# Attention with a ring of three PSUM pairs: another order of maxima and scores in rounds 3 to 5 of a unit

## The chip, the cores and the metric

The kernel runs on one core of a Trainium2 chip. The metric is the device time of one execution in microseconds (us), the median of the runs. The trace is one profiled execution. TensorE does matrix multiplies into PSUM, VectorE (DVE) and ScalarE (ACT) read PSUM and compute elementwise, GpSimd (POOL) works on SBUF alone, and SyncE (SP) issues the transfers. Each engine takes its instructions in order and waits on semaphores that others raise.

## What is computed

The reference is one block of a hybrid network on x of shape (2, 1024, 128):

```python
x = x + attention(layernorm(x))      # 16 heads of 64, causal; values are the keys; then @ W_out
x = x + mixture(layernorm(x))        # 16 experts of width 64, top 2, and a shared one
x = x + state_space(layernorm(x))    # inner width 256, 64 states, convolution of 3 taps, a scan
x = x + mixture(layernorm(x))

# attention, per batch and head
scores = (q / 8) @ k.T ; scores = where(causal, scores, -max)
attn = softmax(scores) ; out = attn @ k
```

The change touches only the attention, the first of the four stages.

## The kernel before

**Units.** `attention` (line 239) works in 16 units (`UNITS`). A unit is one pair of heads and one batch entry: 1024 queries by 1024 keys for two heads at once. The two heads lie in the two halves of the 128 partitions, so most matmuls come in pairs that run beside each other (x2 in the rows).

**What a unit needs.** The softmax subtracts a row maximum before the exponential. So each unit has two kinds of score computation. *Maxima* (`max_scores`, line 582, matmul on line 590) compute coarse scores with queries as rows, into PSUM, in ten fills M0 to M9 (`MAX_FILLS`). VectorE reduces each fill (`maxima`, line 488): where the fill crosses the diagonal it uses a scan with a mask for each head (line 498, followed by a small read of the accumulator), else one plain maximum (line 494). Maxima 2 and 5 are fills of 384 columns for each head, 1, 3, 4, 6, 7 and 9 of 512, 0 and 8 of 128 + 256. *Scores* (`scores`, line 603, matmuls on lines 616, 618, 620, 623, 625) compute exact scores with keys as rows, in nine fills S0 to S8 (`SLOTS`). The rows are high and low parts of queries and keys multiplied in three steps (616, 618, 620), a mask on diagonal tiles (623) and the subtraction of the row maximum (625). ScalarE takes the exponential of each fill (line 453). Maxima run one unit ahead: while unit u has its scores, unit u + 1 has its maxima.

**After the maxima.** `join_maxima` (line 504, instruction on line 507) reduces all maxima of a unit, TensorE turns the result (`turn_max`, line 595, matmul on line 600), and VectorE makes rows of it (line 512), which the scores of the next unit use.

**Rest of a unit.** Output matmuls (`outputs`, line 629, matmul on line 643) multiply the exponentials of the unit before by its keys, one burst at the start of each round. GpSimd adds up exponentials (line 378), TensorE turns the sums into denominators (`denominators`, line 649, matmul on line 656), at the start of rounds 2 and 4. Queries and keys of later units are projected (`project`, line 559, lines 567 to 569): queries in round 1, keys at the end of round 5. Keys are turned in round 1 (line 578).

**The ring.** Scores, maxima, projections and turned keys share one ring of three pairs of PSUM banks. `ring_uses` (line 223) lists all uses in the order of TensorE's work; use number i takes pair i modulo 3, and `pair_free` (line 286) makes TensorE wait until use i - 3 has been read: scores by ScalarE's exponential, maxima by VectorE, key projections by ScalarE.

**What sets the order.** The table `ROUNDS` (lines 211 and 212), written by hand. A unit has five rounds, one for each entry. TensorE, ScalarE and VectorE all walk through it; ScalarE takes the S entries, VectorE the M entries, TensorE both. In the last unit there are no M entries, since no unit follows. The output burst of a round comes before its row of the table.

Of the kernel before, what the change touches and what calls it, by code (L numbers as in the profile page):

```python
# [99 lines left out]
def layernorm_transposed(nc, s, k, load, banks, xn, sync_first, vector_first, gpsimd_work):  # L100
# [85 lines left out]
    def later(piece):  # L186
        def issue(eng):
# [20 lines left out]

BURSTS = [[(0, 0), (1, 0), (2, 0), (1, 1)], [(3, 0), (2, 1)], [(4, 0)], [(5, 0), (6, 0)], [(7, 0), (8, 0), (8, 1)]]
NBURST = len(BURSTS)  # L210
ROUNDS = [[("S", 0)], [("S", 1), ("M", 0), ("S", 2), ("M", 1)], [("S", 3), ("M", 2), ("S", 4), ("M", 3), ("M", 4)],
          [("S", 5), ("M", 5), ("S", 6), ("M", 6), ("M", 7)], [("M", 8), ("S", 7), ("M", 9), ("S", 8)]]
FIRST_OF_HALF = {0: 0, 1: 1}
BURST_OF = [max(r for r, b in enumerate(BURSTS) if any(s == slot for s, _ in b)) for slot in range(NSLOT)]

# [7 lines left out]
def ring_uses():  # L223

    uses = [("K", 0, 0), ("Q", 0, 0), ("T", 0, 0)] + [("M", 0, m) for m in range(NMAX)] + [("K", 1, 0)]
    for unit in range(UNITS):
        more = unit + 1 < UNITS
        for r, row in enumerate(ROUNDS):
            if r == 0 and more:
# [9 lines left out]
def attention(nc, k, w_qk, load_x, load_w_out):  # L239
# [3 lines left out]
    with Scope(nc, "at") as s:  # L243
# [113 lines left out]
        with nc.Block() as block:  # L357
# [57 lines left out]
            def _(act):  # L415
# [46 lines left out]
                for unit in range(UNITS):  # L462
                    more = unit + 1 < UNITS
                    for r, row in enumerate(ROUNDS):
                        if r == 0 and more:
# [15 lines left out]
            def _(dve):  # L481
# [50 lines left out]
                for unit in range(UNITS):  # L532
                    more = unit + 1 < UNITS
                    for r, row in enumerate(ROUNDS):
                        if r == 0:
# [22 lines left out]
            def _(pe):  # L558
# [112 lines left out]
                for unit in range(UNITS + 1):  # L671
                    more = unit + 1 < UNITS
                    for r, row in enumerate(ROUNDS):
                        if r == 0 and unit < UNITS:
# [987 lines left out]
```

How the kernel before makes its waits and increments, by code:

```python
def wait(eng, sem, value):  # L46
    if not isinstance(value, int) or value > 0:
        eng.wait_ge(sem, value)
# [32 lines left out]
def row_statistics(dve, stats, moments, x, small, count, done):  # L82
    for t in range(x.shape[1]):
        last = dve.bn_stats(stats[:, t, :], x[:, t, :])
    last.then_inc(small, 1)
    dve.wait_ge(small, count + 1)
    for t in range(x.shape[1]):
        last = dve.bn_aggr(moments[:, t, :], stats[:, t, :])
    last.then_inc(done, 1)
    return count + 1
# [26 lines left out]
    def norm(eng, n):  # L118
        eng.wait_ge(inverted, n + 1)
        scale_rows(eng, grp(xn, n), grp(k.x, n), grp(moments, n), cols(rstd, n), normed)
# [1 line left out]
    def turn(pe, n):  # L122
        pe.wait_ge(normed, n + 1)
        for j in range(PER):
            last = pe.transpose(tp[n % EARLY][:, j * P:(j + 1) * P], xn[:, n * PER + j, :], k.ident[:, :])
        last.then_inc(transposed, 1)
# [1 line left out]
    def high_part(act, n):  # L128
        act.wait_ge(transposed, n + 1)
        act.activation(k.xhi[:, n * BANK:(n + 1) * BANK], tp[n % EARLY][:, :], ACT.Copy).then_inc(high, 1)
# [1 line left out]
    def low_part(dve, n):  # L132
        dve.wait_ge(high, n + 1)
        c = slice(n * BANK, (n + 1) * BANK)
        dve.tensor_tensor(k.xlo[:, c], tp[n % EARLY][:, :], k.xhi[:, c].bitcast(FP32), ALU.subtract).then_inc(low, 1)
# [15 lines left out]
            def statistics(n):  # L151
                dve.wait_ge(x_loaded[n], 16)
                count[0] = row_statistics(dve, grp(stats, n), grp(moments, n), grp(k.x, n), small, count[0], varied)
```

## Time and profile before

| | before |
|---|---|
| median of 3 runs | 817.79 us (816.99 to 819.50) |
| profiled execution | 819.88 us |
| its span, first to last instruction | 818.1 us |
| mean granted clock of TensorE | 0.971 of full speed |
| TensorE busy (matmuls) | 746.5 us, 91% of the span |
| VectorE busy | 451.1 us, 55% |
| ScalarE busy | 386.0 us, 47% |
| GpSimd busy | 424.1 us, 52% |

The attention takes a bit less than the first 500 us of the span. Its sixteen units begin with the turned row maximum (line 600): unit 0 at 37.49 us, unit 6 at 209.58, unit 15 at 466.87. In the timelines a row gives the start in us from the begin of the span, the duration in us, the engine, line and operation, the tiles written and read, the shape, and how many instructions were merged into the row; in brackets the idle time of the engine before it and who ended it. A matmul's duration overlaps the next one's, so distances between starts tell more than durations. For weight loads (PEld) the list of waits has rows of its own.

### The profile page before, as it was taken

How to read it: one execution, taken by the hardware profiler on the slowest of the kernel's cores; microseconds unless marked ns; L12 is line 12 of the kernel's file. 1: busy time of each engine (PE TensorE's matmuls, PEld its weight loads, DVE VectorE, ACT ScalarE, POOL GpSimd, SP SyncE). 2: the span in 40 equal slices, each digit the busy share in tenths (PEclk: the TensorE clock that was granted, in tenths of full speed). 3: DMA queues.
4: the chain of work that ended last, by engine and by line, in shares of the span. 5: the costliest groups of instructions: out<-in, count | busy, mean ns of one | idle time of the engine just before them, and what ended most of it. 6: DMA issues, size and time to landing. Idle time of an engine off the chain costs nothing. (4 is left out here: it accounts for less than half of the span.)

```text
span 818.1 us, 14386 instructions
## 1 busy us (share of the span) xinstructions
PE 746.5 (91%) x5520; PEld 507.0 (62%) x5520; DVE 451.1 (55%) x1218; ACT 386.0 (47%) x476; POOL 424.1 (52%) x309
## 2 busy tenths in 40 slices
PE   2689999999999999999999998979799897779998
PEld 1456555655655565565556555958688763657887
DVE  5755665675567557556655701553554457555342
ACT  2346555555554555555455451355354344364421
POOL 4346775685676658658655862133544321144343
PEclk9789999999999999999999999999899899899999
DMA  2000000000000000000000004332222000033232
GB/s 64 8 1 1 9 1 1 8 1 1 9 1 2 7 1 2 8 1 2 1 2 26 1 2 101 92 105 78 69 80 90 1 1 0 1 111 112 71 100 78
DMA packets 29752, 25.56 MB, mean 31 GB/s; under 512 B 10162, under 2 KB 21236, under 8 KB 29684
## 3 DMA queue, kind: packets, MB, share of 16 engines
q1 hardware_dynamic: 29684, 24.64, 10.0%
q8 instruction: 44, 0.72, 0.4%
q14 instruction: 24, 0.20, 0.1%
HBM read 23.32 MB, written 1.31 MB: 30 GB/s over the span
## 5 line engine op out<-in xcount | busy, mean ns | idle before, releaser
L378 POOL TENSOR_TENSOR all_x<-all_x,at_probs 128x1024 f32<-128x1024 f32 (+3 forms) x128 | 221.7, 1732 | 35.7 <-ACT at_probs L453 21.1
L453 ACT ACTIVATE at_probs<-at_ring 128x1024 f32<-128x1024 f32 x144 | 147.2, 1024 | 113.6 <-PE at_ring L625 106.9
L498 DVE CUSTOM_DVE_ANT_0 at_ring<-at_ring,at_after_query 128x128 f32<-128x128 f32 (+3 forms) x256 | 119.5, 521 | 74.3 <-PE at_ring L590 74.3
L643 PE MATMUL at_out<-at_probs,at_k_nat 128*64 128x512 f32 (+3 forms) x768 | 140.3, 494 | 1.1 <-DVE a_attn_t L521 0.9
L1079 POOL TENSOR_TENSOR m_prod<-m_gate,m_wb 128x512 f32<-128x512 f32 x64 | 82.0, 1287 | 111.9 <-ACT m_gate L936 87.2
L378 POOL TENSOR_TENSOR all_x<-at_probs 128x768 f32<-128x768 f32 (+1 forms) x32 | 67.0, 2092 | 128.2 <-ACT at_probs L453 128.0
L990 DVE TENSOR_TENSOR m_hid<-m_prod,m_u 128x512 f32<-128x512 f32 x64 | 44.0, 687 | 90.0 <-POOL m_prod L1079 84.6
L643 PEld LDWEIGHTS at_out<-at_probs,at_k_nat 128*64 128x64 f32 x768 | 49.2, 136 | 69.9 <-issue 66.0
L494 DVE TENSOR_REDUCE at_half_max<-at_ring 128x2 f32<-128x1024 f32 x64 | 75.5, 1222 | 12.3 <-PE at_ring L590 12.3
L936 ACT ACTIVATE m_gate<-m_g 128x512 f32<-128x512 f32 x72 | 42.8, 598 | 81.9 <-PE m_g L847 81.5
L855 PEld LDWEIGHTS m_acc<-rest_wd,m_hid 128*128 128x128 f32 x576 | 76.7, 195 | 6.1
L616 PE MATMUL at_ring<-at_qh,at_kh 64*128 64x512 f32 (+3 forms) x384 | 73.6, 380 | 5.7 <-DVE at_m_rows L512 2.2
L855 PE MATMUL m_acc<-rest_wd,m_hid 128*128 128x128 f32 x576 | 76.8, 278 | 0.0
L625 PE MATMUL at_ring<-at_m_rows,at_ones_r 64*128 64x512 f32 (+3 forms) x384 | 75.9, 391 | 0.0
L590 PE MATMUL at_ring<-at_kh,at_qh 64*128 64x512 f32 (+3 forms) x384 | 64.2, 383 | 10.0 <-DVE at_half_max L498 3.0
L616 PEld LDWEIGHTS at_ring<-at_qh,at_kh 64*128 64x128 f32 x384 | 36.6, 187 | 52.6 <-issue 37.5
L618 PE MATMUL at_ring<-at_ql,at_kh 64*128 64x512 f32 (+3 forms) x384 | 66.9, 344 | 0.0
L620 PE MATMUL at_ring<-at_qh,at_kl 64*128 64x512 f32 (+3 forms) x384 | 66.8, 344 | 0.0
L590 PEld LDWEIGHTS at_ring<-at_kh,at_qh 64*128 64x128 f32 x384 | 35.9, 187 | 30.2 <-issue 26.8
L485 DVE TENSOR_TENSOR at_ql<-at_ring,at_qh 128x1024 fp32r<-128x1024 f32 x16 | 19.6, 1224 | 55.9 <-ACT at_qh L429 55.9
L444 ACT ACTIVATE at_inv<-at_misc 128x512 f32<-128x512 f32 x32 | 19.1, 598 | 65.3 <-PE at_misc L656 65.3
L620 PEld LDWEIGHTS at_ring<-at_qh,at_kl 64*128 64x128 f32 x384 | 36.4, 186 | 4.3
(218 smaller groups left out, 1289.4 us busy)
## 6 DMA issues: line engine op xcount, KB each, us to landing
m_wb<-m_wt_far SPq DMA_DIRECT2D x128, 128.0 KB, 2.9
all_x<-in_L_attn_a_x SPq DMA_DIRECT2D x8, 256.0 KB, 4.0
at_w_raw<-in_L_attn_a_W_qk SPq DMA_DIRECT2D x8, 128.0 KB, 2.6
out<-all_x SPq DMA_DIRECT2D x4, 256.0 KB, 3.3
a_room<-in_L_attn_a_W_out SPq DMA_DIRECT2D x1, 512.0 KB, 4.0
m_raw_wg<-in_L_ffn_experts_wg SPq DMA_DIRECT2D x1, 512.0 KB, 4.2
m_raw_wu<-in_L_ffn_experts_wu SPq DMA_DIRECT2D x1, 512.0 KB, 4.1
rest_wd<-in_L_ffn_experts_wd SPq DMA_DIRECT2D x1, 512.0 KB, 4.2
```

The costliest lines, as they stand in the source:

```text
L378: return pool.tensor_tensor(sums[:, :, a * P:b * P], left, right, ALU.add)
L453: act.activation(probs[:, :, slot * BANK:(slot + 1) * BANK], pair("S", unit, slot)[:, :, :], ACT.Exp, scale=BETA).then_inc(exp_done, 1)
L494: last = dve.reduce_max(half_max[:, :, i, out], pair("M", unit, m)[:, :, at:at + w], AX.X)
L498: last = dve.tensor_tensor_reduce(out=sums_ps, in0=sums_ps, in1=after_query[:, BANK - w:BANK], scale=1.0, scalar=MASKED, op0=ALU.add, op1= ...
L590: last = pe.matmul(out[:, l, at:at + (b - a) * P], qh[u][rows(l), i * P:(i + 1) * P], kh[u][rows(l), a * P:b * P], start=True, stop=True)
L616: pe.matmul(to[l], kh[u][rows(l), keys], qh[u][rows(l), q], start=True, stop=False)
L618: pe.matmul(to[l], kh[u][rows(l), keys], ql[u][rows(l), q], start=False, stop=False)
L620: pe.matmul(to[l], kl[u][rows(l), keys], qh[u][rows(l), q], start=False, stop=False)
L625: last = pe.matmul(to[l], ones_r[rows(l), :], m_rows[u][rows(l), q], start=False, stop=True)
L643: last = pe.matmul(out_ps[rows(l), o:o + (b - a) * P], k_nat[g % 3][:, j, rows(l)], probs[:, l, at:at + (b - a) * P], start=(j == 0), stop ...
L855: last = pe.matmul(acc[:, t * P:(t + 1) * P], hid[g % BUFS][:, t * P:(t + 1) * P], f.wd[:, st, :], start=(st == 0 and t == 0), stop=(st == ...
L1079: pool.tensor_tensor(prod[g % BUFS][:, :], gate[g % BUFS][:, :], wb[q % SPREAD][:, :], ALU.mult)\
```

## The change

Rounds 3 and 4 begin with a maxima fill instead of a scores fill, and in round 5 scores 7 go ahead of maxima 8. The instructions are the same, in the same number; `ring_uses` follows the table, so each fill's place in the ring and its wait follow too.

```diff
-ROUNDS = [[("S", 0)], [("S", 1), ("M", 0), ("S", 2), ("M", 1)], [("S", 3), ("M", 2), ("S", 4), ("M", 3), ("M", 4)],
-          [("S", 5), ("M", 5), ("S", 6), ("M", 6), ("M", 7)], [("M", 8), ("S", 7), ("M", 9), ("S", 8)]]
+ROUNDS = [[("S", 0)], [("S", 1), ("M", 0), ("S", 2), ("M", 1)], [("M", 2), ("S", 3), ("M", 3), ("S", 4), ("M", 4)],
+          [("M", 5), ("S", 5), ("M", 6), ("S", 6), ("M", 7)], [("S", 7), ("M", 8), ("M", 9), ("S", 8)]]
```

## Rows read from the trace of the kernel before

**Rows 1.** Busy time by window: us, then each engine, clock, DMA; unit 6.
```profile
210.00:238.75 28.75, 28.30 (x244) 16.58 (x240) 17.59 (x42) 15.63 (x19) 19.72 (x14) 1.00 0.02 6
```

**Rows 2.** List of waits, 40 to 520 us: us in total, times, longest.
```profile
PEld at_ring L616 <- DVE at_half_max L498: 9.5, 16, 1.0
...
PE at_ring L590 <- ACT at_probs L453: 2.6, 15, 0.3
```

**Rows 3.** Timeline (start, us, ..., idle before), TensorE, unit 6, rounds 2 and 3.
```profile
220.91 0.39 PE L590 MATMUL at_ring<-at_kh,at_qh 64*128 64x512 f32 x2
221.22 1.08 PE L643 MATMUL at_out<-at_probs,at_k_nat 128*64 128x512 f32 x4
222.23 0.50 PE L616 MATMUL at_ring<-at_qh,at_kh 64*128 64x512 f32 x2
222.57 0.40 PE L618 MATMUL at_ring<-at_ql,at_kh 64*128 64x512 f32 x2
...
223.28 0.34 PE L590 MATMUL at_ring<-at_kh,at_qh 64*128 64x384 f32 x2
...
224.68 0.79 PE L590 MATMUL at_ring<-at_kh,at_qh 64*128 64x512 f32 x4
225.40 1.94 PE L643 MATMUL at_out<-at_probs,at_k_nat 128*64 128x512 f32 x8
```

**Rows 4.** Timeline, VectorE, unit 6, rounds 2, 3 and 5.
```profile
222.63 0.14 DVE L498 DVE_READ_ACCUMULATOR2_ANT at_half_max<- 128x1 f32 x1
223.69 0.57 DVE L498 CUSTOM_DVE_ANT_0 at_ring<-at_ring,at_after_query 128x384 f32<-128x384 f32 x1 [0.92 <-PE at_ring L590]
...
224.69 0.14 DVE L498 DVE_READ_ACCUMULATOR2_ANT at_half_max<- 128x1 f32 x1
...
234.95 0.14 DVE L498 DVE_READ_ACCUMULATOR2_ANT at_half_max<- 128x1 f32 x1
```

**Rows 5.** Timeline, TensorE, unit 6, rounds 4 and 5.
```profile
228.13 0.50 PE L616 MATMUL at_ring<-at_qh,at_kh 64*128 64x512 f32 x2
...
231.28 1.94 PE L643 MATMUL at_out<-at_probs,at_k_nat 128*64 128x512 f32 x12
233.15 0.50 PE L590 MATMUL at_ring<-at_kh,at_qh 64*128 64x128 f32 x4
233.49 0.39 PE L616 MATMUL at_ring<-at_qh,at_kh 64*128 64x512 f32 x2
...
234.60 0.40 PE L590 MATMUL at_ring<-at_kh,at_qh 64*128 64x512 f32 x2
235.14 0.45 PE L616 MATMUL at_ring<-at_qh,at_kh 64*128 64x384 f32 x2
...
236.75 0.50 PE L567 MATMUL at_ring<-all_xhi,at_w_hi 128*128 128x512 f32 x1
```

**Rows 6.** Timeline, ScalarE, unit 6, rounds 3 and 5.
```profile
223.51 2.13 ACT L453 ACTIVATE at_probs<-at_ring 128x1024 f32<-128x1024 f32 x2 [1.35 <-PE at_ring L625]
...
234.83 1.03 ACT L453 ACTIVATE at_probs<-at_ring 128x1024 f32<-128x1024 f32 x1 [3.31 <-PE at_ring L625]
```

**Rows 7.** Timeline, TensorE, unit 0, rounds 3, 4 and 5.
```profile
52.45 0.44 PE L590 MATMUL at_ring<-at_kh,at_qh 64*128 64x384 f32 x2
...
54.87 1.08 PE L656 MATMUL at_misc<-all_x,at_ones 128*64 128x512 f32 x4 [0.16 <-POOL all_x L378]
55.88 0.50 PE L616 MATMUL at_ring<-at_qh,at_kh 64*128 64x512 f32 x2
...
64.17 0.50 PE L567 MATMUL at_ring<-all_xhi,at_w_hi 128*128 128x512 f32 x1
```

**Rows 8.** Timeline, VectorE, unit 0, end of maxima 1.
```profile
52.77 0.14 DVE L498 DVE_READ_ACCUMULATOR2_ANT at_half_max<- 128x1 f32 x1
```

**Rows 9.** Timeline, VectorE, unit 14, the row maximum.
```profile
466.62 0.19 DVE L507 TENSOR_REDUCE at_row_max<-at_half_max 128x16 f32<-128x32 f32 x1
```

**Rows 10.** Timeline, TensorE, start of unit 15.
```profile
466.87 0.44 PE L600 MATMUL at_misc<-all_ident,at_row_max 128*64 128x128 f32 x4
```

## The prediction

> **What bounds the kernel now.** I read the busy time of a window first, then the list of waits, then the timelines of TensorE, VectorE and ScalarE through one unit. In a window as long as one attention unit TensorE is busy 28.30 of 28.75 us at a granted clock of 1.00, while VectorE, ScalarE and GpSimd are busy 17.6, 15.6 and 19.7 us [rows 1]. TensorE sets the pace, so only what its queue waits for, or what makes it restart, can move the time. The period is steady: from the key projection that ends unit 0 (64.17) to the same one of unit 6 (236.75) it is 172.58 / 6 = 28.76 us [rows 5, 7].
>
> The waits name two holds that come back about once a unit: TensorE behind VectorE's maxima (9.5 us over 16 times, seen at the weight load) and behind ScalarE's exponentials (2.6 us, 15 times, of what the engine shows as idle) [rows 2]. Both are the ring of three PSUM pairs: a use may be written only when the use three places earlier has been read. I write S for a scores fill, M for a maxima fill, and X<-Y for "X waits until Y is read".
>
> First the speed without waits. The first matmul step of scores 3 takes 222.57 - 222.23 = 0.34 us, the three after it (223.28 - 222.57) / 3 = 0.24 each [rows 3]. So scores without a mask take 4 x 0.24 = 0.95 in a stream and 1.05 behind output matmuls or after a wait: a restart costs 0.10. A maxima fill of 512 columns takes 0.24, one of 384 columns three quarters of it, 0.18.
>
> Then the holds. Maxima 3 start at 224.68, though maxima 2 and scores 4 before them end at 223.28 + 0.18 + 0.95 = 224.41. They wait 0.27 us for the exponential of scores 3 (M3<-S3), which runs 223.51 to 224.54; the fill follows it by 0.14 [rows 3, 6]. Round 4 has the same (M6<-S5). In round 5 scores 8 wait for maxima 8: VectorE reads their last part until 235.09, scores 8 start at 235.14, 0.05 later, and 0.3 after maxima 9 (234.60 + 0.24) [rows 4, 5].
>
> **The change, part by part.** Nothing is added or removed, no DMA is moved or passed, and the order within M and within S stays, so VectorE's and ScalarE's orders stay too. What changes is TensorE's order, and with it who stands three places ahead. Now: M3<-S3, S4<-M1, M6<-S5, S6<-M4, S8<-M8. Afterwards: S4<-M2, M4<-S3, S6<-M5, M7<-S5, S7<-M6, M8<-S6, S8<-S7, and the projection K<-M8.
>
> *Round 3.* Now it takes 225.40 - 222.23 = 3.17 us from its first fill to the output matmuls of the next round [rows 3]. Afterwards maxima 2 stand first. From the start of that fill to VectorE's last read of it is 224.83 - 223.28 = 1.55 us [rows 3, 4]; for the place behind the outputs I add the 0.10. VectorE is there in time: maxima 1 end at 222.77 [rows 4], and the new fill would be readable 0.41 + 0.10 after 222.23. Scores 4 start 1.55 + 0.10 + 0.05 = 1.70 after the round's start. Under that lie maxima 2, scores 3 and maxima 3, 0.28 + 0.95 + 0.24 = 1.47, so TensorE idles 0.23. Then scores 4 with a restart, 1.05, and maxima 4 with the turn to the outputs, 221.22 - 220.91 = 0.31 as in round 2: 1.70 + 1.05 + 0.31 = 3.06. M4<-S3 doesn't bind: scores 3 end at 0.28 + 0.95, ScalarE starts 0.23 later (223.51 - 223.28), and 1.03 + 0.14 more give 2.63, before scores 4 end at 2.75. Gain 0.11.
>
> *Round 4.* Maxima 5 have the size of maxima 2, so again 3.06, against 231.28 - 228.13 = 3.15 now [rows 5]. Gain 0.09.
>
> *Round 5.* Now 236.75 - 233.15 = 3.60 from maxima 8 to the projection. Afterwards scores 7 stand first, and scores 8 need their exponential: from scores 7's start to ScalarE's 234.83 - 233.49 = 1.34, plus 0.10 behind the outputs, the exponential 1.03, the handover 0.14: 2.61 before scores 8 may start [rows 5, 6]. Under it lie scores 7 (234.60 - 233.49 + 0.10 = 1.21), maxima 8 (0.34 or less, 233.15 to 233.49) and maxima 9 (0.24), 1.79 in all. So TensorE idles 0.82 where it now idles 0.3. Scores 8 up to the projection take 236.75 - 235.14 = 1.61 with their restart. Together 4.22, a loss of 0.62. K<-M8 is free by then: VectorE's last read of maxima 8 comes 235.09 - 233.15 = 1.94 after that fill starts, so at 1.21 + 1.94 = 3.15.
>
> *The steady unit:* 0.62 - 0.11 - 0.09 = +0.42 us, for 13 units (1 to 13): +5.5.
>
> *Unit 0* has no outputs between its rounds. Scores 3 take over the wait that maxima 2 have now, for the exponential of scores 2, and start at 52.45 [rows 7]. VectorE ends maxima 1 at 52.91 [rows 8] and needs 1.14 for maxima 2 (223.69 to 224.83), so scores 4 start at 54.10 and the denominators at 54.10 + 1.05 + 0.31 = 55.46, now 54.87. They take 1.01 as now (55.88 - 54.87), round 4 takes 1.70 + 1.05 + 0.24, round 5 1.34 + 1.03 + 0.14 + 1.61 = 4.12: the projection at 63.58, now 64.17 [rows 7]. Unit 0: -0.6.
>
> *Unit 14* has no projection behind scores 8, and its row maximum sets the turn: VectorE ends it at 466.81, TensorE goes on at 466.87 [rows 9, 10]. VectorE gets maxima 8 later by scores 7's 1.21, less the 0.2 gained before: +1.0. Unit 15 has scores alone, in the same order: 0.
>
> *Sum:* 5.5 - 0.6 + 1.0 = +5.9 us. The profiled execution took 819.88 (span 818.1 and 1.8 around it) and would take 825.8. It lies 2.1 above the median of the runs, 817.79, so in medians the forecast is 817.79 + 5.9 = 823.7.
>
> *Costed at nothing.* GpSimd's sums follow the exponentials; GpSimd is busy 19.7 us of 28.75 and gets the seventh exponential a little sooner. Without that cover the denominators would wait for it. The row maximum ends up to 1 us later, but the projection, six steps of 0.24, stands before its use in all but unit 14, where it is charged.
>
> *Bounds.* Above: the two early maxima fills are each released 0.1 later than 1.70, as VectorE's handover could be 0.14 like ScalarE's: rounds 3 and 4 gain nothing, the unit is +0.62, the sum 8.1 - 0.3 + 1.2 = +9.0. Below: VectorE releases them as soon as TensorE gets there, and both idles and restarts vanish; then each round takes 0.28 + 0.95 + 0.24 + 0.95 + 0.31 = 2.73, the unit is 0.62 - 0.44 - 0.42 = -0.24, and the sum 13 x -0.24 - 0.9 + 0.2 = -3.8. I take +5.9: 1.55 is measured on the same fill, and stands nearer to the upper end.
>
> *The restart.* Where scores 8 wait now, the weight load itself is what waits (L616, 16 times) [rows 2], and the restart of 0.10 follows. The Trainium skill, page "TensorE: Matmul & The Clock Gate", section "Architectural detail: the array is 16x 32x32, not 1x 128x128", says that TensorE's queue can pull weight loads ahead of matmuls in flight. If that reached past a semaphore wait, scores 4 and 6 would restart free and the sum would be 14 x 0.2 = 2.8 lower, +3.1. The row speaks against it, so the restart stays in.
>
> **The rivals.**
> *R1, faster:* the lower bound as a mechanism. Place: S4<-M2 and S6<-M5. It decides when VectorE releases within 1.47 us of the round's start instead of 1.70. Then the 0.44 that each pair of last maxima loses now (0.27 of wait and 225.40 - 224.68 - 0.55 = 0.17 of restart) is all gained, and scores 8's wait doesn't eat it: 817.8 - 3.8 = 814. For it: VectorE is busy only 17.6 of 28.75 us. Against: the 1.55 are one fill and two scans behind each other, and no queue that could get shorter.
> *R2, no change:* the new wait of scores 8 is given back by slack further on. For it: the projection and the turn after it leave VectorE and ScalarE idle. Against: TensorE's idle time is under 0.5 us of a window, so there is no slack on the engine that counts. If half of the 0.42 were absorbed in each unit and unit 14 cost 0.5: 13 x 0.21 - 0.6 + 0.5 = +2.6, just at the edge; with all of it, 0. I put 819.
> *R3, slower still:* the maxima, read a microsecond later, go round the ring: the turn of the next unit's keys needs maxima 9 read, and the row maximum the same. For it: unit 14 has no room there at all. Against: projection and outputs lie between. If 0.4 us a unit showed: 14 x 0.4 = 5.6 more, 829.
>
> **How the numbers follow.** Forecast 0.80, R1 0.05, R2 0.08, R3 0.07. A difference under 0.3% (2.5 us) can't be told from none here. Slower by more than that: 0.80 + 0.07 less 0.02 for the forecast's low tail = 0.85; within it 0.08 + 0.02 less 0.01 = 0.09; faster 0.05 + 0.01 = 0.06. The forecast's own range, with 0.15 us either way on each steady unit, is 821.5 to 826.5. Taking in part of the bounds and the spread between executions (816.99 to 819.50): 820 to 827.5.
>
> **What would show it.** In the trace after: scores 8 released by ScalarE 2.6 us after scores 7's start, and TensorE idle 0.8 before them; 3.06 us in rounds 3 and 4, with scores 4 and 6 released by VectorE and no wait before maxima 4 and 7; a period of 29.18 us. If scores 8 start within 2.2 us of scores 7, or the period is under 28.9, the step of round 5 is wrong. If rounds 3 and 4 come under 2.9, R1's mechanism holds. A period right and a time wrong would put the error in unit 0, in unit 14 or behind the attention.

## The result, and the profile after

| | before | after |
|---|---|---|
| median | 817.74 us (816.99 to 819.50, 8 runs) | 822.26 us (820.04 to 824.41, 8 runs) |
| ratio | 1 | 1.0052, 95% interval 1.0036 to 1.0068 |
| profiled execution / span | 819.88 / 818.1 us | 820.70 / 818.9 us |
| start of unit 0, 1, 14, 15 | 37.49, 65.77, 439.70, 466.87 | 37.63, 64.33, 442.92, 470.94 |
| steady unit, mean of 1 to 13 | 28.76 us | 29.12 us |
| unit 0 / unit 14 | 28.29 / 27.16 us | 26.70 / 28.01 us |
| from the start of unit 15 to the end | 351.2 us | 348.0 us |

The change makes the kernel 0.52% slower, 4.5 us in the medians. The two profiled spans differ by 0.8 us only, and that is no contradiction: the profiled execution before lies 2.1 us above its median and the one after 1.6 us below its own. In the trace unit 15 starts 4.1 us later after the change, but the stages behind the attention, which have the same instructions in the same order, were 3.2 us shorter. The window 540 to 800 us shows what differed there. The columns are us, busy us of TensorE, its weight loads, VectorE, ScalarE and GpSimd, the granted clock, and the transfers. Before:

```profile
540.00:800.00 260.00, 230.71 (x1282) 187.35 (x1281) 137.27 (x424) 114.14 (x157) 98.44 (x79) 0.94 0.20 65
```

After, with the window of one whole unit above it:

```profile
210.00:239.12 29.12, 28.24 (x243) 16.45 (x242) 17.80 (x42) 15.74 (x18) 19.63 (x14) 1.00 0.02 6
540.00:800.00 260.00, 227.20 (x1285) 184.10 (x1286) 139.85 (x433) 117.82 (x160) 98.39 (x79) 0.97 0.21 65
```

The granted clock was 0.97 of full speed there instead of 0.94, and TensorE was busy 3.5 us less with nearly the same number of matmuls (1285 against 1282). So the attention has to be read unit by unit, and not by the difference of two spans. In the unit TensorE is busy 28.24 of 29.12 us where it was 28.30 of 28.75 [rows 1]: the same work in a longer period at the same clock of 1.00.

TensorE in unit 6 after the change, rounds 3 to 5 and the start of unit 7 (start, duration, idle time before in brackets; it answers to [rows 3, 5]):

```profile
222.62 0.45 PE L590 MATMUL at_ring<-at_kh,at_qh 64*128 64x384 f32 x2
...
223.83 0.40 PE L590 MATMUL at_ring<-at_kh,at_qh 64*128 64x512 f32 x2
224.32 0.50 PE L616 MATMUL at_ring<-at_qh,at_kh 64*128 64x512 f32 x2
...
225.36 0.40 PE L590 MATMUL at_ring<-at_kh,at_qh 64*128 64x512 f32 x2
225.69 1.94 PE L643 MATMUL at_out<-at_probs,at_k_nat 128*64 128x512 f32 x8
...
228.42 0.44 PE L590 MATMUL at_ring<-at_kh,at_qh 64*128 64x384 f32 x2
...
231.49 1.94 PE L643 MATMUL at_out<-at_probs,at_k_nat 128*64 128x512 f32 x12
233.36 0.50 PE L616 MATMUL at_ring<-at_qh,at_kh 64*128 64x512 f32 x2
...
234.58 0.62 PE L590 MATMUL at_ring<-at_kh,at_qh 64*128 64x128 f32 x6
235.88 0.44 PE L616 MATMUL at_ring<-at_qh,at_kh 64*128 64x384 f32 x2 [0.68 <-ACT at_probs L453]
...
237.48 0.50 PE L567 MATMUL at_ring<-all_xhi,at_w_hi 128*128 128x512 f32 x1
...
239.08 0.44 PE L600 MATMUL at_misc<-all_ident,at_row_max 128*64 128x128 f32 x4
```

Round 3 runs from 222.62 to 225.69, 3.07 us instead of 3.17. Maxima 3 end at 223.83 + 0.24 = 224.07 and scores 4 start at 224.32: 0.25 us of idle time that was not there. But maxima 4 (225.36) follow scores 4 without a wait. Round 4 takes 231.49 - 228.42 = 3.07 instead of 3.15. Round 5 takes 237.48 - 233.36 = 4.12 instead of 3.60: maxima 8 and 9 (the row of six matmuls at 234.58) are through by 235.10, and scores 8 wait until 235.88. The row of scores 8 names ScalarE's exponential as what ended the wait.

VectorE, the last reads of maxima 1, maxima 2 and maxima 8 (the answer to [rows 4]):

```profile
223.01 0.14 DVE L498 DVE_READ_ACCUMULATOR2_ANT at_half_max<- 128x1 f32 x1
...
224.13 0.14 DVE L498 DVE_READ_ACCUMULATOR2_ANT at_half_max<- 128x1 f32 x1
...
236.27 0.14 DVE L498 DVE_READ_ACCUMULATOR2_ANT at_half_max<- 128x1 f32 x1
```

It ends maxima 2 at 224.27, 0.05 before scores 4 start. It ends maxima 8 at 236.41, when scores 8 have been running for 0.53 us, so maxima 8, which held them before the change, hold them no more. ScalarE, the exponential of scores 7 (the answer to [rows 6]):

```profile
234.81 1.02 ACT L453 ACTIVATE at_probs<-at_ring 128x1024 f32<-128x1024 f32 x1 [2.39 <-PE at_ring L625]
```

It ends at 235.83, and the weight load of scores 8 starts 0.05 later. The list of waits shows the new picture as a whole (us in total, times, longest): VectorE now holds the scores about twice a unit for half a microsecond at the weight load, ScalarE once a unit for a whole one.

```profile
PEld at_ring L616 <- DVE at_half_max L498: 16.2, 30, 0.7
PEld at_ring L616 <- ACT at_probs L453: 15.9, 16, 1.1
...
PE at_ring L616 <- ACT at_probs L453: 10.6, 16, 0.7
```

### The profile page after: what moved, and what is told of

It is laid out like the page before. It is cut to its first block and busy times, and to the rows that moved or that the text cites. A ratio compares the mean times of both kernels' runs of the same rounds, so it can differ in the third digit from the quotient of the medians.

```text
span 818.9 us, 14386 instructions
## 1 busy us (share of the span) xinstructions
PE 739.8 (90%) x5520; PEld 500.5 (61%) x5520; DVE 454.5 (56%) x1218; ACT 387.6 (47%) x476; POOL 417.2 (51%) x309
## 5 line engine op out<-in xcount | busy, mean ns | idle before, releaser
L378 POOL TENSOR_TENSOR all_x<-all_x,at_probs 128x1024 f32<-128x1024 f32 (+3 forms) x128 | 208.6, 1630 | 26.1 <-ACT at_probs L453 11.3
L494 DVE TENSOR_REDUCE at_half_max<-at_ring 128x2 f32<-128x1024 f32 x64 | 78.3, 1225 | 9.8 <-PE at_ring L590 9.0
```

Source lines behind the costliest of these rows:

```text
L378: return pool.tensor_tensor(sums[:, :, a * P:b * P], left, right, ALU.add)
L494: last = dve.reduce_max(half_max[:, :, i, out], pair("M", unit, m)[:, :, at:at + w], AX.X)
```

## The experiments

Every kernel below ran in turn with the kernel before, whose median beside it is in the column "before". The numbers 1 to 8 are the experiments. "Period" is the mean of units 1 to 13 from the starts of the turned row maximum.

| kernel | period | unit 14 | median | before | ratio, 95% interval |
|---|---|---|---|---|---|
| before | 28.76 | 27.16 | | | |
| the change | 29.12 | 28.01 | 822.26 | 817.74 | 1.0036 to 1.0068 |
| 1: rounds 3 and 4 alone | 28.58 | 27.00 | 814.66 | 817.78 | 0.9942 to 0.9973 |
| 2: round 5 alone | 29.30 | 28.19 | 825.28 | 817.78 | 1.0075 to 1.0109 |
| 3: change, denominators under scores 8's wait | 28.50 | 27.15 | 813.30 | 817.78 | 0.9922 to 0.9953 |
| 4: rounds 3 and 4 alone, output burst moved | 29.22 | 27.62 | 824.19 | 817.78 | 1.0060 to 1.0090 |
| 5: as 3, second denominators under scores 4's wait | 28.51 | 27.15 | 813.70 | 817.36 | 0.9948 to 0.9974 |
| 6: as 1, both denominators under VectorE's waits | 28.57 | 26.96 | 815.23 | 817.36 | 0.9956 to 0.9979 |
| 7: before, one semaphore for each maxima fill | 28.58 | 26.98 | 814.19 | 817.36 | 0.9940 to 0.9972 |
| 8: 5 and 7 together | 28.51 | 27.15 | 812.53 | 817.36 | 0.9931 to 0.9957 |

**1 and 2: the two halves of the change.**

```diff
 # 1, against the kernel before
-... [("S", 3), ("M", 2), ("S", 4), ("M", 3), ("M", 4)], [("S", 5), ("M", 5), ("S", 6), ("M", 6), ("M", 7)], ...
+... [("M", 2), ("S", 3), ("M", 3), ("S", 4), ("M", 4)], [("M", 5), ("S", 5), ("M", 6), ("S", 6), ("M", 7)], ...
 # 2, against the kernel before
-... [("M", 8), ("S", 7), ("M", 9), ("S", 8)]]
+... [("S", 7), ("M", 8), ("M", 9), ("S", 8)]]
```

> Rounds 3 and 4 of the change alone, round 5 in the old order. Theory (the loss sits in round 5, where scores 8 wait for the exponential of scores 7; rounds 3 and 4 gain about 0.09 us each): rounds 3 and 4 take 3.07 us each, round 5 again 3.60, period 28.58 us instead of 28.76, time about 3 us under before: 814.8. Rival A (maxima first costs by itself, through the two new waits of scores 4 and 6 behind VectorE): period above 28.76, time 818 or more. Rival B (the loss goes round the ring from one unit to the next): period above the sum of its rounds.

> Round 5 of the change alone (scores 7 ahead of maxima 8), rounds 3 and 4 in the old order. Theory: round 5 takes 4.12 us instead of 3.60, the period is 28.76 + 0.52 = 29.28 us, unit 14 is about 1 us longer because its row maximum ends later, unit 0 about unchanged: 13 x 0.52 + 1 = +7.8, 825.5. Rival A (rounds 3 and 4 cost): period 28.76 or less, no loss. Rival B (round the ring): the loss is more than the sum of the rounds, over 829.

TensorE in the first: the starts of rounds 3, 4 and 5, the outputs behind rounds 3 and 4, and the projection.

```profile
221.16 0.45 PE L590 MATMUL at_ring<-at_kh,at_qh 64*128 64x384 f32 x2
...
224.23 1.94 PE L643 MATMUL at_out<-at_probs,at_k_nat 128*64 128x512 f32 x8
...
226.96 0.45 PE L590 MATMUL at_ring<-at_kh,at_qh 64*128 64x384 f32 x2
...
230.03 1.94 PE L643 MATMUL at_out<-at_probs,at_k_nat 128*64 128x512 f32 x12
231.90 0.49 PE L590 MATMUL at_ring<-at_kh,at_qh 64*128 64x128 f32 x4
...
235.50 0.50 PE L567 MATMUL at_ring<-all_xhi,at_w_hi 128*128 128x512 f32 x1
```

Rounds 3 and 4 take 3.07 each, round 5 takes 235.50 - 231.90 = 3.60 as before. The period falls by 0.18 and the time by 3.1 us (ratio 0.9957). The second, round 5 from scores 7 to the projection:

```profile
234.88 0.50 PE L616 MATMUL at_ring<-at_qh,at_kh 64*128 64x512 f32 x2
...
237.40 0.44 PE L616 MATMUL at_ring<-at_qh,at_kh 64*128 64x384 f32 x2 [0.68 <-ACT at_probs L453]
...
239.00 0.50 PE L567 MATMUL at_ring<-all_xhi,at_w_hi 128*128 128x512 f32 x1
```

It takes 4.12 us, and the period is 28.76 + 0.54. The time rises by 7.5 us. So the change is a gain and a loss that were bundled: 0.18 us a unit won in rounds 3 and 4, 0.54 lost in round 5, 0.36 in sum, which is the period after the change. Rival A (maxima first costs) falls, as the first kernel has the shorter period. Rival B (the delay goes round the ring) falls too, as the period is the sum of its rounds in both, within 0.02 us.

**3: is the wait before scores 8 empty time?**

TensorE's part; ScalarE's inversion of the denominators moves likewise, to the place before the exponential of scores 8.

```diff
+DEN_BEFORE = {8: 0}
...
-                        if r == 3:
-                            denominators(unit, 0)
...
                             if what == "S":
+                                if DEN_BEFORE.get(n) == 0:
+                                    denominators(unit, 0)
...
                                 scores(unit, n)
```

> The changed kernel, with the denominators of the unit's first half (0.86 us of TensorE work) taken from the start of round 4 and put right before scores 8, under their wait; ScalarE's inversion goes before the exponential of scores 8 to match. Theory (0.78 us of pure idle time stands before scores 8, TensorE has nothing else that it may do there): the 0.86 us vanish into it but for 0.17 with the turn between the two kinds of matmul, the period falls by 0.69 to 28.43 us, the time to about 812. Rival (the wait is not set by scores 7's exponential but by something that moves along, as VectorE's maxima 8 or the order on ScalarE): the wait grows again, the period stays at 29.0 or more, the time at 821 or more.

```profile
230.03 0.50 PE L619 MATMUL at_ring<-at_qh,at_kh 64*128 64x512 f32 x2
...
231.24 0.63 PE L593 MATMUL at_ring<-at_kh,at_qh 64*128 64x128 f32 x6
231.80 1.08 PE L659 MATMUL at_misc<-all_x,at_ones 128*64 128x512 f32 x4
232.81 0.44 PE L619 MATMUL at_ring<-at_qh,at_kh 64*128 64x384 f32 x2
...
234.41 0.50 PE L570 MATMUL at_ring<-all_xhi,at_w_hi 128*128 128x512 f32 x1
```

The denominators (line 659 here) now run from 231.80 to 232.81, and scores 8 follow them with no wait: they start 2.78 us after scores 7, and the exponential had needed 2.52. The period falls from 29.12 to 28.50, by 0.62 of the 0.69 expected. The wait was filled with work of another kind, so TensorE had been empty there, and what set the wait did not move along with the denominators. The changed kernel with this one move is 0.6% faster than the kernel before.

**4: a cover that was one already.** The kernel is that of experiment 1, with this edit:

```diff
-                        if unit:
+                        if unit and (r != 2 or unit == UNITS):
                             outputs(unit - 1, r)
...
                             if what == "S":
+                                if n == 4 and unit:
+                                    outputs(unit - 1, 2)
                                 scores(unit, n)
```

> Rounds 3 and 4 of the change with the old round 5, and in round 3 the output burst (four pairs of matmuls, about 1 us) moved from the round's start to the place before scores 4, where TensorE waits for VectorE's maxima 2. Theory (0.23 us of idle time and one restart of 0.10 are there to be had): from maxima 1 to the next outputs 4.05 us instead of 4.40 with the change, period 28.58 - 0.35 = 28.23 us, time about 810. Rival (the restart and the wait come back at another place, as maxima 2 directly behind maxima 1 make VectorE late): period 28.5 or more, time 814 or more.

This was wrong by 14 us. TensorE from maxima 1 and 2 (the row of four matmuls) over scores 3 and the moved burst to the next outputs:

```profile
222.76 0.88 PE L590 MATMUL at_ring<-at_kh,at_qh 64*128 64x512 f32 x4
224.07 0.50 PE L616 MATMUL at_ring<-at_qh,at_kh 64*128 64x512 f32 x2 [0.42 <-ACT at_probs L453]
...
225.44 1.08 PE L643 MATMUL at_out<-at_probs,at_k_nat 128*64 128x512 f32 x4
...
227.81 1.94 PE L643 MATMUL at_out<-at_probs,at_k_nat 128*64 128x512 f32 x8
```

The wait before scores 4 did go. But scores 3 start at 224.07, though maxima 1 and 2 end at 222.76 + 0.42 = 223.18: 0.89 us of waiting for the exponential of scores 2. S3<-S2 is in the ring in every kernel that has maxima 2 first (in the kernel before it is M2<-S2), and from unit 1 on the output burst between rounds 2 and 3 had covered it. The expectation named only the wait that it meant to fill. From maxima 1 to the outputs it took 5.05 us instead of the 4.05 worked out, the 0.89 and a restart. Unit 0, which has no output burst, shows the same wait in the kernel after, before scores 3, and the prediction had used it there.

**5 and 6: the smaller waits.**

```diff
 # 5, against 3: the second half's denominators go from round 2 to scores 4
-DEN_BEFORE = {8: 0}
+DEN_BEFORE = {8: 0, 4: 1}
 # 6, against 1: the same, and the first half's go to scores 6
+DEN_BEFORE = {6: 0, 4: 1}
 # both, TensorE's part (ScalarE's inversions move likewise)
-                        if r == 1 and unit:
+                        if r == 1 and unit == UNITS:
                             denominators(unit - 1, 1)
...
                             if what == "S":
...
+                                if DEN_BEFORE.get(n) == 1 and unit:
+                                    denominators(unit - 1, 1)
                                 scores(unit, n)
```

> The changed kernel with both denominators moved under waits: those of the first half right before scores 8 (as in the run before), those of the second half from round 2 to the place before scores 4, where 0.25 us of idle time stand behind maxima 2. Theory (a denominator costs 0.86 us where it follows outputs and 1.01 between two fills, and hides what it stands under): 28.50 + 0.15 - 0.25 = 28.40 us a unit, about 811.8. Rival (as with the output burst, what moves away was the cover of another wait, here scores 1 or 2 in round 2): a new wait in round 2, period 28.7 or more, 816 or more.

> Rounds 3 and 4 of the change with the old round 5, and both denominators under the two waits behind VectorE: the second half's before scores 4, the first half's before scores 6. Theory: 28.58 + 2 x (0.15 - 0.25) = 28.38 us a unit, about 811.7. Rival (ScalarE's inversion now stands between the exponentials of scores 5 and 6 and makes maxima 8 or scores 7 late): period 28.6 or more, 815 or more.

Neither made a difference to the kernel it builds on (28.51 against 28.50, 28.57 against 28.58), so both expectations missed, by 0.11 and 0.19 us a unit. Maxima 3, the denominators and scores 4 in experiment 5:

```profile
220.90 0.40 PE L591 MATMUL at_ring<-at_kh,at_qh 64*128 64x512 f32 x2
221.23 1.08 PE L657 MATMUL at_misc<-all_x,at_ones 128*64 128x512 f32 x4
222.24 0.50 PE L617 MATMUL at_ring<-at_qh,at_kh 64*128 64x512 f32 x2
```

From maxima 3 to scores 4 it is 1.34 us, where it was 224.32 - 223.83 = 0.49: 0.85 more, as much as round 2 lost. The denominators cost 1.10 between two fills (1.34 less the fill's 0.24) and not the 1.01 that I put: they start 0.33 after maxima 3, where a fill behind a fill starts after 0.24, and scores 4 start 1.01 after them. Behind outputs they cost 0.86. So the wait of 0.25 is hidden and 0.24 is paid for it. The wait of 0.78 before scores 8 left a gain, this one doesn't. The feared new waits didn't come either.

**7 and 8: one semaphore or two.**

```diff
-                    pe.wait_ge(hi_done, 2 * unit + 2)
+                    if m == 0:
+                        pe.wait_ge(hi_done, 2 * unit + 2)
                     pair_free(pe, "M", unit, m)
```

> The kernel before, but the maxima fills 1 to 9 of a unit no longer wait a second time for the queries' high part, which the first fill has waited for; so each maxima fill has one semaphore to wait for and not two. Theory (with two waits the ring's wait is an instruction of its own in front of the weight load, 0.11 us from the end of the exponential to the load, where scores fills with the wait on the load itself need 0.05): the holds of maxima 3 and 6 shrink by 0.06 to 0.09 each, period 28.60 us instead of 28.76, time about 815.4. Rival (ScalarE hands over later than VectorE, whoever waits): the period stays at 28.76.

> Both denominators under waits, as in the first of these four runs, with one semaphore for each maxima fill as in the third. Theory (the single wait pays only where a maxima fill is what TensorE waits with, and here these are all scores fills): the same period as the first of these runs within 0.05 us, 28.40, about 811.8. Rival (two waits cost at every maxima fill, waiting or not): period lower by 0.3 or more, 807.

The rows are the weight load (PEld) with which a wait for ScalarE ends. Before: maxima 3, whose exponential ended at 224.54 [rows 6].

```profile
224.65 0.51 PEld L590 LDWEIGHTS at_ring<-at_kh,at_qh 64*128 64x128 f32 x4 [0.54 <-issue]
```

After the change: scores 8, whose exponential ended at 235.83.

```profile
235.88 0.19 PEld L616 LDWEIGHTS at_ring<-at_qh,at_kh 64*128 64x128 f32 x2 [1.00 <-ACT at_probs L453]
```

Experiment 7: maxima 3 again, with one semaphore to wait for; the first fill of the unit has already waited for the other. First ScalarE's two exponentials merged into one row (the first lasts 1.03, as all do, so to 223.81), then the load.

```profile
222.78 2.13 ACT L453 ACTIVATE at_probs<-at_ring 128x1024 f32<-128x1024 f32 x2 [1.35 <-PE at_ring L626]
```

```profile
223.86 0.48 PEld L591 LDWEIGHTS at_ring<-at_kh,at_qh 64*128 64x128 f32 x4 [0.48 <-ACT at_probs L453]
```

The gap from exponential to load is 0.11, 0.05 and 0.05 us. With a single semaphore the maxima fill starts as promptly as the scores fill, so the handover depends on how many semaphores the waiting instruction has, not on which engine releases. The period falls to 28.58, 0.18 less for two waits of this kind a unit, and the time by 3.2 us. Of the 0.09 for each wait 0.06 is the load that starts sooner; the rest is the maxima's first matmul, which starts with its load (both at 223.86) and not 0.03 behind it (224.68 against 224.65).

TensorE in round 3 of experiment 7, scores 3 and the outputs behind the round:

```profile
221.50 0.51 PE L617 MATMUL at_ring<-at_qh,at_kh 64*128 64x512 f32 x2
...
224.58 1.94 PE L644 MATMUL at_out<-at_probs,at_k_nat 128*64 128x512 f32 x8
```

Round 3 takes 3.08 us in the old order, and with maxima first it took 3.07: experiments 1 and 7 reach the same period, 28.58, by different ways. So what the new order won in rounds 3 and 4 is no more than what the second semaphore had cost there. The two gains don't add up: beside the new order one semaphore wins nothing (experiment 8, below). The new order with one semaphore and no denominators moved was not run.

Experiment 8 has the period of experiment 5, 28.51: where only scores fills wait, the second semaphore of the maxima costs nothing that shows. Its median is 1.2 us lower than that of experiment 5, but the two profiled spans are 810.9 and 810.8 us, so no gain is shown. It has the lowest median of all kernels here; against experiment 3 (813.30) the difference isn't clear of noise.

## Why the prediction was right

Forecast 823.7 us, slower; measured 822.26.

- *Rounds 3 and 4* were worked out to 3.06 each and take 3.07. Scores 4 start 224.32 - 222.62 = 1.70 us into the round, the value of the sum. What carried it was a latency read whole from the rows, from the start of a fill to VectorE's last read of it.
- *Round 5* was put at 4.22 and takes 4.12. The start of the exponential was right (1.44 forecast, 234.81 - 233.36 = 1.45), its length too. The term that was mis-sized is the handover: 0.14 taken from a maxima fill, 0.05 in fact, as experiment 7 explains. Maxima 8 were put at 0.34 and took 0.28, which made no difference, as they lie under the wait. The steady unit loses 0.36 instead of 0.42: round 5 is 0.10 under the forecast, rounds 3 and 4 are 0.01 over it each, and 0.02 is not in these rounds. That is 0.8 us of the sum.
- *The restart* of 0.10 stood in for scores 4: they take 225.36 - 224.32 = 1.04 and not 0.95, though their weight load had waited. The Trainium skill's rule on weight loads pulled ahead of matmuls in flight ("TensorE: Matmul & The Clock Gate", section "Architectural detail: the array is 16x 32x32, not 1x 128x128") does not reach past a semaphore here: the load of scores 8 begins at the release, at 235.88, and not before it.
- *Unit 0.* TensorE in rounds 3, 4 and 5, scores 3, denominators and projection, the answer to [rows 7]:

```profile
51.61 0.50 PE L616 MATMUL at_ring<-at_qh,at_kh 64*128 64x512 f32 x2 [0.74 <-ACT at_probs L453]
...
54.62 1.08 PE L656 MATMUL at_misc<-all_x,at_ones 128*64 128x512 f32 x4
...
62.73 0.50 PE L567 MATMUL at_ring<-all_xhi,at_w_hi 128*128 128x512 f32 x1
```

  From scores 3 to the denominators it takes 3.01, from there to the projection 8.11; forecast 55.46 - 52.45 = 3.01 and 63.58 - 55.46 = 8.12. From maxima 1 to the projection it is 0.7 us less than before, where 0.6 was forecast; the 0.1 is scores 3, which start 1.30 behind maxima 1, where maxima 2 had started 1.40 behind them. But unit 0 is 1.6 us shorter in the profile. The other 0.9 lies before maxima 1, where the order is the same. The windows from 37.5 to 50 us, before and then after:

```profile
37.50:50.00 12.50, 9.43 (x73) 6.39 (x72) 4.01 (x8) 6.05 (x7) 0.00 (x0) 0.60 0.01 1
```

```profile
37.50:50.00 12.50, 8.99 (x85) 6.19 (x84) 4.83 (x12) 5.99 (x7) 0.72 (x1) 0.82 0.00 1
```

  The granted clock was 0.60 before and 0.82 after. From the start of unit 0 to maxima 1 it is 13.56 us before and 12.68 after. Over all ten profiles here it is 12.7 to 12.8 us where this window's clock was 0.80 to 0.84, and 13.0 to 13.6 where it was 0.60 to 0.72; experiments 5 and 8, with the same order up to there, are 13.56 at 0.60 and 12.72 at 0.84. So this part goes with the clock of the single execution and not with the change, and the forecast had nothing for it.
- *Unit 14* was put at +1.0 and is +0.85. VectorE's row maximum, then TensorE's turn, the answer to [rows 9, 10]:

```profile
470.69 0.18 DVE L507 TENSOR_REDUCE at_row_max<-at_half_max 128x16 f32<-128x32 f32 x1
```

```profile
470.94 0.44 PE L600 MATMUL at_misc<-all_ident,at_row_max 128*64 128x128 f32 x4 [0.41 <-DVE at_row_max L507]
```

  TensorE waits 0.41 us for it where it did not before.
- *The sum.* From the trace: 13 x 0.36 + 0.85 - 0.7 = +4.8 us, forecast +5.9, measured +4.5 with an interval of 2.9 to 5.6. The forecast's total is 1.4 us over the measured median, and 0.8 of it is the steady unit, from the handover; 0.3 is unit 14 and unit 0, and the last 0.3 is below what medians that spread over 2 to 4 us can tell. Which rounds gain, which one loses and by what wait came out as worked. One step of the working doesn't come out: 0.15 us on each of 13 units is 2.0, which gives 821.7 to 825.7 and not 826.5 at the upper end.
- *The rivals.* R1 (VectorE releases early enough) fails on the 1.70, R2 (slack further on) on a period that is the sum of its rounds, R3 (round the ring) likewise in experiment 2. That scores 7's exponential sets the wait rests on the row that names it, on the 0.05 us between its end and the load, on VectorE reading maxima 8 until after scores 8 have started, and on experiment 3; a shorter exponential wasn't tried.

## What to carry to other kernels

In a ring of buffers a new order is judged by writing for each use which one stands a ring's length ahead, and comparing the time from that one's start to its release with the work that lies between; do this for every use, those too whose wait doesn't show, since something may be covering them (experiment 4). A table changed in several places is a bundle: each row is priced alone and the gain and the loss kept apart. Long waits are worth filling with work moved from elsewhere, short ones only if the move costs less than they do; and an instruction on the critical queue should wait for one semaphore where a second can be proven by order.

## What the runs showed of the hardware

- A second semaphore on a TensorE instruction that truly waits delayed its weight load by 0.06 us (0.11 against 0.05), and lengthened the period by 0.09 for each such wait (28.76 against 28.58 for two). Where the instruction didn't have to wait, it cost nothing that shows (28.51 against 28.51).
- Denominator matmuls cost more between two fills than behind output matmuls: 1.10 us between maxima and scores (experiment 5), 0.86 behind outputs.
- Stages with the same instructions in the same order differed by up to 3.4 us between profiled runs (from unit 15 to the end 347.8 to 351.2 us), with the granted clock in the window 540 to 800 us at 0.94 to 0.97. At a change worth 4 us a single span is a poor guide (here it showed 0.8); the period of a repeated unit, which stayed within 0.02 us of its mean inside each run, is a good one.
